# A transformer block with two mixture-of-experts FFNs on one core: the first FFN computed by chosen token-expert pairs

## The reference

```
x = x + wavelet_attention(layernorm(x))
x = x + ffn(layernorm(x))              # the FFN that the change touches
x = x + attention(layernorm(x))        # local, top-k and global keys
x = x + ffn(layernorm(x))

def ffn(x, Wg, W1, W2):                # 8 experts, D = 128, H = 256
    probs = softmax(x @ Wg); top_w, top_i = top_k(probs, 2)
    top_w = top_w / (sum(top_w) + 1e-8)
    combine = one_hot weights of the two chosen experts, else 0
    h = square(relu(einsum('td,edh->teh', x, W1)))
    y = einsum('teh,ehd->ted', h, W2)
    return einsum('te,ted->td', combine, y)
```

## Time and profile before

| | us |
|---|---|
| median of 2 runs | 679.55 (676.53 to 682.57) |
| the profiled execution | 683.03 |
| its span, first to last instruction | 681.1 |
| TensorE's mean granted clock in it, as a share of 2.4 GHz | 0.946 |

### The profile page before, as it was taken

The page is one execution under the profiler, slowest core; times in us unless marked ns, Lnnn a source line. Parts: engine busy times, 40 slices in busy tenths (PEclk is TensorE's granted clock), DMA queues, the critical chain, the costliest instruction groups (busy, mean ns, idle before and its releaser), DMA issues.

```text
span 681.1 us, 13634 instructions
## 1 busy us (share of the span) xinstructions
PE 606.3 (89%) x4874; PEld 378.8 (56%) x4874; DVE 429.0 (63%) x1449; ACT 336.5 (49%) x697; POOL 227.6 (33%) x386
## 2 busy tenths in 40 slices
PE   6799888888795866999999998999989989999997
PEld 3376566466474553555555554555445436677776
DVE  2446755744744788777777877787777536654554
ACT  5434432522431200567776667767646764445543
POOL 1121111321341309766666854787501001000000
PEclk9979999989888895799999999999989999999999
DMA  8000000000000000000000000000000000000000
GB/s 259 18 1 1 1 0 1 0 1 0 2 0 1 10 0 12 13 13 14 13 14 12 11 14 12 13 8 11 9 12 12 3 1 0 1 17 15 1 16 17
DMA packets 13171, 9.52 MB, mean 14 GB/s; under 512 B 5168, under 2 KB 12720, under 8 KB 12848
## 3 DMA queue, kind: packets, MB, share of 16 engines
q1 hardware_dynamic: 13104, 8.66, 4.5%
HBM read 4.71 MB, written 1.05 MB: 8 GB/s over the span
## 4 chain that ended last, share of the span: by engine, by line
PE 69%; DVE 23%; issue 5%; ACT 1%; POOL 1%; DMA 0%; SPq 0%; POOLq 0%; DVEq 0%; ACTq 0%
PE BANK L1079 18%; PE BANK L1064 11%; PE BANK L1223 5%; PE BANK L1174 5%; PE BANK L1198 4%; PE BANK L1195 3%; DVE X L808 3%; PE BANK L1180 3%; PE BANK L1226 2%; PE BANK L1229 2%; DVE QST L899 2%; DVE SW L852 2%; PE BANK L1201 2%; DVE M L851 2%; PE BANK L968 2%
## 5 line engine op out<-in xcount | busy, mean ns | idle before, releaser
L610 ACT ACTIVATE PT<-BANK 128x256 f32<-128x256 f32 (+2 forms) x352 | 156.9, 493 | 92.7 <-PE BANK L1198 75.3
L388 POOL TENSOR_SCALAR OH<-IOTA,POS 128x128 bf16<-128x128 bf16 x240 | 139.5, 602 | 33.3 <-DVE POS L860 28.8
L1079 PEld LDWEIGHTS BANK<-W,HID 128*128 128x128 f32 x1024 | 133.2, 206 | 28.0 <-issue 14.2
L537 ACT ACTIVATE RELU<-BANK 128x512 f32<-128x512 f32 x128 | 76.2, 596 | 141.1 <-PE BANK L1064 140.6
L808 DVE SCALAR_TENSOR_TENSOR X<-BANK,COMB,X 128x128 f32<-128x128 f32 x256 | 72.1, 344 | 116.7 <-PE BANK L1079 116.7
L1079 PE MATMUL BANK<-W,HID 128*128 128x128 f32 x1024 | 136.5, 292 | 7.6 <-DVE HID L797 7.6
L1064 PE MATMUL BANK<-XNT_ALL,W 128*128 128x512 f32 x256 | 122.8, 607 | 0.0
L894 DVE CUSTOM_DVE_ANT_0 XN_a<-BANK,BANDQ 128x256 f32<-128x256 f32 (+1 forms) x128 | 62.6, 489 | 38.9 <-PE BANK L1174 38.8
L894 DVE CUSTOM_DVE_ANT_0 XN_c<-BANK,BANDQ 128x384 f32<-128x384 f32 (+1 forms) x128 | 62.4, 488 | 9.6 <-PE BANK L1174 8.6
L1064 PEld LDWEIGHTS BANK<-XNT_ALL,W 128*128 128x128 f32 x256 | 44.8, 198 | 37.9 <-issue 28.2
L1195 PE MATMUL BANK<-BANDK,IDB 128*128 128x128 bf16 x384 | 64.2, 222 | 0.3
(11 more groups left out here) (230 smaller groups left out, 901.4 us busy)
## 6 DMA issues: line engine op xcount, KB each, us to landing
W<-w SPq DMA_DIRECT2D x2, 1024.0 KB, 8.0
X<-x SPq DMA_DIRECT2D x4, 256.0 KB, 3.1
out<-X SPq DMA_DIRECT2D x4, 256.0 KB, 2.2
RELU<-KALL SPq DMA_DIRECT2D x20, 36.0 KB, 1.9
HID<-KALL SPq DMA_DIRECT2D x20, 36.0 KB, 1.9
ROW<-rows SPq DMA_DIRECT2D x1, 320.0 KB, 3.1
RELU<-KALL SPq DMA_DIRECT2D x20, 8.0 KB, 1.7
HID<-KALL SPq DMA_DIRECT2D x20, 8.0 KB, 1.7
```

The lines of the kernel that those rows point to most:

```text
L388: last = nc.gpsimd.tensor_scalar(OH[g % 2][:, i, t, :], IOTA[:, :], POS[:, t, c:c + 1], None, ALU.is_equal)
L537: nc.scalar.activation(RELU[u % 4][:, :], UP_BANK[hh][:, :], ACT.Relu).then_inc(s["relu"], 1)
L610: nc.scalar.activation(PT[u % PT_RING][:, 0:w], P2_BANK[u % SCORE_RING][:, 0:w], ACT.Exp, scale=SCALE).then_inc(S["exp_done"], 1)
L1079: last = mm(DOWN_BANK[e % 2][:, t * P:(t + 1) * P], HID_T[e % 2][:, hh, t * P:(t + 1) * P], W2[:, e, hh, :], start=(hh == 0), stop=(hh == ...
```

## The change

The first FFN no longer loops over experts for all tokens. The sequences are taken in two waves of two. In each wave there are 2048 pairs of a token and a chosen expert.

- `choices` (DVE, step 7) writes each token's two weights into the normalised rows XROW (130 wide: 128 channels, the weight, the number of the pair); ScalarE makes the second copy of the rows. `positions` (TensorE, step 7) counts with triangular matmuls how many tokens before this one chose the same expert, `slots` (DVE, step 8) turns it into a row of the DRAM tensor XS, which has a region for each expert, and GpSimd scatters the rows there in 16 indirect DMAs a wave. `table` (DVE, step 9 of the wave's second sequence) lists for each of the 23 tiles its region row and its expert; 23 tiles of 128 rows always suffice.
- SyncE reads each tile's two numbers from SBUF into registers and loads its rows from DRAM and its expert's weights (256 KB, from SBUF to SBUF: W1 and W2 now lie together as W12) into a ring of four. A tile is then: `tile_turn` (transpose), `tile_copy`, `tile_up`, `tile_hidden` (ReLU and square, both ScalarE), `tile_down`, `tile_y` (DVE: times the weight, and the number of the pair as an index), `tile_out` (GpSimd: an indirect DMA to YT in DRAM).
- When all tiles of a wave are out, `sums_in` loads the two rows of each token, and `add_experts` adds them to X.
- The steps of `a_step` run two sequences at a time, two steps apart (`pair`): for sequences 0 and 1 ahead of wave 0; for 2 and 3 the first four ahead of it and the others beside its tiles. They share banks, so steps have new waits for the copies of the other sequence, as `pe.wait_ge(S["a_coef_s"], sent["a_coef"])` in step 0. The steps of `c_step` for sequences 0 and 1 run beside wave 1, those of 2 and 3 after it. `keep_busy` is cut to three matmuls after each pair of steps.
- At the start SyncE fills both XS with zeros, 4.33 MB each, behind the loads of the inputs.
- On GpSimd `stacks` and `values` of sequences 0 and 1 stand behind the last `tile_out`, ahead of `rstd("c", 2)`.

The second FFN and all that follows are as before. The core of the diff (the steps' new waits, `table`, `positions` and the instructions of TensorE for a tile, which are as described, are left out):

```diff
+WAVE = 2
+JT = WAVE * T
+NT = (2 * JT * P + E * (P - 1)) // P
+REGION = JT * P
+SLOTS = E * REGION + P
+ROW_W = D + 2
+UNUSED = 4096
+A_STEPS = 10
+LAG = 2
+IN_RING = 4
...
+def pair(k, b):
+    return [(s, x) for s, x in ((k, b), (k - LAG, b + 1)) if 0 <= s < A_STEPS]
...
+A_LAST = A_STEPS + LAG
+A_AHEAD = 4
+def beside_tile(i):
+    return pair(A_AHEAD + i // 2, WAVE) if i % 2 == 0 and A_AHEAD + i // 2 < A_LAST else []
+def c_beside_tile(i):
+    return [(s, b) for s, b in ((i + 3, 0), (i - 5, 1)) if (3 if b == 0 else 0) <= s <= 3 + T]
...
+            sp.wait_ge(S["act_zero1"], 1)
+            per = SLOTS * ROW_W // P
+            reps = 13
+            for w in range(B // WAVE):
+                none = QST[1][:].rearrange("p t h c -> p (t h c)").bitcast(F32)[:, 0:per // reps]
+                sp.dma_start(XS[w][:, :].rearrange("r c -> (r c)").rearrange("(p k n) -> p k n", p=P, k=reps),
+                             none.unsqueeze(1).to_broadcast([P, reps, per // reps])).then_inc(ZEROED[w], 16)
+            def tiles_in(w):
+                sp.wait_ge(S["r_table"], w + 1)
+                sp.wait_ge(S["scattered"], 16 * 2 * JT * (w + 1))
+                for n in range(w * NT, (w + 1) * NT):
+                    i, slot = n - w * NT, n % IN_RING
+                    row = sp.value_load(TABLE[0:1, w, 0, i:i + 1], min_val=0, max_val=E * JT)
+                    e = sp.value_load(TABLE[0:1, w, 1, i:i + 1], min_val=0, max_val=E - 1)
+                    if n >= IN_RING:
+                        sp.wait_ge(S["tile_y"], n - IN_RING + 1)
+                    sp.dma_start(XT_IN[slot], XS[w][:, :].rearrange("(r p) c -> p r c", p=P)[:, bass.DynSlice(row, 1), :]
+                                 .rearrange("p r c -> p (r c)")).then_inc(TILE_IN[slot], 16)
+                    sp.dma_start(WST[slot][:, :], W12[:, bass.DynSlice(e, 1), :].rearrange("p e c -> p (e c)")
+                                 ).then_inc(TILE_IN[slot], 16)
+            def sums_in(b):
+                w = b // WAVE
+                if b % WAVE == 0:
+                    for slot in range(IN_RING):
+                        sp.wait_ge(Y_OUT[slot], 16 * slot_count(slot, (w + 1) * NT))
+                if b >= 2:
+                    sp.wait_ge(S["x_sum"], b - 1)
+                for k in range(2):
+                    first = k * JT * P + b % WAVE * L
+                    sp.dma_start(YB[b % 2][k], YT[w][first:first + L, :].rearrange("(t p) d -> p t d", p=P)
+                                 ).then_inc(Y_IN[b % 2], 16)
+            for w in range(B // WAVE):
+                tiles_in(w)
+                for b in range(w * WAVE, (w + 1) * WAVE):
+                    sums_in(b)
...
+            def scatter(b, n):
+                w, j, k = b // WAVE, b % WAVE * T + n // 2, n % 2
+                if n == 0:
+                    pool.wait_ge(S["r_idx"], b + 1)
+                    pool.wait_ge(S["g_twice"], b + 1)
+                    if b % WAVE == 0:
+                        pool.wait_ge(ZEROED[w], 16)
+                nc.gpsimd.indirect_dma_start(
+                    XS[w][:, :], bass.IndirectOffsetOnAxis(ap=IDX[:, k, j:j + 1], axis=0), XROW[:, k, j, :], None,
+                    bounds_check=SLOTS - 1, oob_is_err=False).then_inc(S["scattered"], 16)
+            def tile_out(n):
+                slot = n % IN_RING
+                pool.wait_ge(S["tile_y"], n + 1)
+                nc.gpsimd.indirect_dma_start(
+                    YT[n // NT][:, :], bass.IndirectOffsetOnAxis(ap=IDY[:, slot:slot + 1], axis=0), YST[slot], None,
+                    bounds_check=2 * JT * P - 1, oob_is_err=False).then_inc(Y_OUT[slot], 16)
...
+            with_bias(1, 0).then_inc(S["a_xb"], 1)
+            consts()
+            rstd("g", 0)
+            ones()
+            rstd("g", 1)
+            rstd("a", 2)
+            pool.wait_ge(S["a_x1"], 1)
+            with_bias(2, 0).then_inc(S["a_xb"], 1)
+            for n in range(2 * T):
+                scatter(0, n)
+            for n in range(2 * T):
+                scatter(1, n)
+            rstd("a", 3)
+            pool.wait_ge(S["a_x1"], 2)
+            with_bias(3, 0).then_inc(S["a_xb"], 1)
+            rstd("g", 2)
+            for i in range(NT):
+                if i == 3:
+                    rstd("g", 3)
+                tile_out(i)
+                if 9 <= i < 9 + 2 * T:
+                    scatter(2, i - 9)
+                if 15 <= i < 15 + 2 * T:
+                    scatter(3, i - 15)
+            rstd("c", 0)
+            for i in range(NT):
+                tile_out(NT + i)
+                if i == 4:
+                    rstd("c", 1)
+            for b in range(2):
+                stacks(b)
+                if b == 0:
+                    for slot in range(IN_RING):
+                        pool.wait_ge(Y_OUT[slot], 16 * slot_count(slot, 2 * NT))
+                values(b)
             pool.wait_ge(S["a_x1"], B)
             for i in range(HG):
                 last = nc.gpsimd.memset(KZ[0][i].bitcast(F32), 0.0)
             last.then_inc(S["heads_zero"], 1)
+            rstd("c", B - 2)
...
+            def tile_copy(n):
+                act.wait_ge(S["tile_t"], n + 1)
+                nc.scalar.copy(XTS[n % 2], T_BANK[:, 0:P]).then_inc(S["tile_xt"], 1)
+            def tile_hidden(n):
+                act.wait_ge(S["tile_up"], n + 1)
+                nc.scalar.activation(TR[n % 2], U_BANK[n % 2][:, 0:HID], ACT.Relu).then_inc(S["tile_relu"], 1)
+                if n >= 2:
+                    act.wait_ge(S["tile_down"], n - 1)
+                act.wait_ge(S["tile_relu"], n + 1)
+                nc.scalar.activation(TH[n % 2], TR[n % 2], ACT.Square).then_inc(S["tile_sq"], 1)
...
+            def choices(b):
+                h = b % WAVE * T
+                ranks("g", b)
+                nc.vector.tensor_scalar(MSK[:, h:h + T, :], GR[:, :, :], 2.0, None, ALU.is_lt).then_inc(S["r_mask"], 1)
+                link(weights(GW[:, :, :]))
+                for k in range(2):
+                    link(nc.vector.scalar_tensor_tensor(out=GK[:, :, :], in0=GR[:, :, :], scalar=float(k), in1=GW[:, :, :],
+                                                        op0=ALU.is_equal, op1=ALU.mult))
+                    link(nc.vector.reduce_sum(XROW[:, k, h:h + T, D], GK[:, :, :], AX_X))
+            def slots(b):
+                h = b % WAVE * T
+                dve.wait_ge(S["r_pos"], b + 1)
+                link(nc.vector.tensor_tensor(GS[:, :, :], R_BANK[:, 0:T * E].rearrange("p (t e) -> p t e", t=T),
+                                             EBASE[:, :].unsqueeze(1).to_broadcast([P, T, E]), ALU.add))
+                for k in range(2):
+                    link(nc.vector.scalar_tensor_tensor(out=GK[:, :, :], in0=GR[:, :, :], scalar=float(k), in1=GS[:, :, :],
+                                                        op0=ALU.is_equal, op1=ALU.mult))
+                    with nc.allow_low_precision(reason="row numbers, whole and below 2 ** 24"):
+                        last = nc.vector.reduce_sum(IDX[:, k, h:h + T], GK[:, :, :], AX_X)
+                    if k == 0:
+                        link(last)
+                last.then_inc(S["r_idx"], 1)
...
+            def tile_y(n):
+                slot = n % IN_RING
+                dve.wait_ge(S["tile_down"], n + 1)
+                if n >= IN_RING:
+                    dve.wait_ge(Y_OUT[slot], 16 * (n // IN_RING))
+                nc.vector.tensor_scalar(IDY[:, slot:slot + 1], XT_IN[slot][:, D + 1:D + 2], float(UNUSED), None, ALU.add)
+                nc.vector.tensor_scalar(YST[slot], D_BANK[:, 0:D], XT_IN[slot][:, D:D + 1], None, ALU.mult).then_inc(S["tile_y"], 1)
+            def add_experts(b):
+                dve.wait_ge(Y_IN[b % 2], 32 * (b // 2 + 1))
+                x = X[:, seq(b), :]
+                link(nc.vector.tensor_tensor(x, x, YB[b % 2][0], ALU.add))
+                nc.vector.tensor_tensor(x, x, YB[b % 2][1], ALU.add).then_inc(S["x_sum"], 1)
...
+            stats("a", 3)
+            for k in range(A_AHEAD):
+                for s, b in pair(k, 2):
+                    a_step(s, b)
+                if k == 0:
+                    normalize("a", 3)
+            for i in range(NT):
+                for s, b in beside_tile(i):
+                    a_step(s, b)
+                tile_y(i)
+            for b in range(2):
+                add_experts(b)
+            for s in range(3):
+                c_step(s, 0)
+            for i in range(NT):
+                for s, b in c_beside_tile(i):
+                    c_step(s, b)
+                tile_y(NT + i)
+            for b in range(2, B):
+                add_experts(b)
+                for s in range(2):
+                    c_step(s, b)
+                if b < B - 1:
+                    for s in range(3, 4 + T):
+                        c_step(s, b)
...
+            def wave(w, beside):
+                n0 = w * NT
+                tile_turn(n0)
+                tile_up(n0)
+                tile_turn(n0 + 1)
```

(8 more changed lines are left out.)

365 lines of the change are left out of this document (255 added, 110 removed).

## The result

| | before | after |
|---|---|---|
| median of 2 runs | 679.55 | 753.86 us (752.95 to 754.76) |
| ratio, 95% interval | | 1.109 (1.087 to 1.131) |
| span of the profiled execution | 681.1 | 753.0 us |
| first MAX8 / from it to the end | 225.2 / 455.9 | 297.1 / 455.9 us |

The direction and the wide range (680 to 775) held. The point, 722, was 32 us too low, and the forecast's own narrower range (695 to 745) was missed. First the page of the changed kernel: the busy line, the granted clock in 40 slices of 18.8 us, and the shares of the chain that ended last.

What follows compares the result with a forecast made beforehand. TensorE's work was taken to bound the first FFN. First tile 72, tiles 115, steps beside 21, gap 15, end 44 sum to MAX8 at 267 us against 225.2, 42 later: 722 us predicted, range 680 to 775.

Steps and rivals of the forecast that it cites:

- the forecast's own narrower range (695 to 745): Whole kernel: the range around the predicted 722 us that the forecast itself claimed, chance 0.50.
- the gap: Between the waves: result scatter, sums' loads, adds, statistics and normalisation leave TensorE standing about 15 us.
- The period, 2.5 us: Each tile of both waves: ring and SyncE together take 2.5 us, 115 us for 46 tiles.
- ring 2.4: Tile loop: load, transpose, down, y, next load take 4.8 us for two tiles, as a ring of two.
- SyncE binds: Rival, tile loop: register loads of 1.2 us and more make 3.5 us a tile, 769 us; chance 0.14.
- loads are not in the loop: Rival, tile loop: fast loads let the period fall to ScalarE's 1.2 to 1.3 us, 666 us; chance 0.11.
- the four steps of batches 2 and 3, some 8 us: Before the first tile: the little work TensorE has during the wait for scatters and load.
- bind only from 1.9: GpSimd in wave 0: 39 indirect DMAs at 1.3 us fit; rival at 1.9 us each, 735 us, chance 0.15.
- The end: Last y to first MAX8: rstd behind stacks, values and memsets, 24.5 us; in all 44.7 against 8.8.
- Beside the tiles: Steps of other batches in the tile loop: 15 us exposed in wave 0, 6 us in wave 1.
- Zero fill free: Start: zeroing 4.33 MB a wave is done at 34 to 55 us, earlier than the last scatter.
- Clock: Waves: TensorE's granted clock falls under 0.8, adding 0.1 to 0.2 us a tile.

Runs made afterwards that it cites:

- e3: Changed kernel with the 46 tiles' rows and experts as constants, so SyncE has no register loads; DMAs the same: 742.3 us.
- e6: Changed kernel with constants for register loads, the transpose of tile i+2 behind tile_down(i), and no 256 KB weight copy: 738.1 us.
- e1: Changed kernel with the rstd of sequence 3 moved on GpSimd between the scatters of sequences 0 and 1: 747.7 us.
- e12: Changed kernel with sequence 3's eight scatters behind the last result scatter of wave 0: 761.0 us.
- e2: Changed kernel with GpSimd's work after the last tile reordered, stacks and values put around the two late rstd, memsets ahead: 744.9 us.
- e10: Changed kernel with the edits of e1, e2 and e12, one register load a tile, and the transpose of tile i+2 behind tile_down(i): 736.1 us, ratio 1.080.
- e13: The edits of e10 without that of e12, on the changed kernel: 735.4 us, ratio 1.082.

## Why the prediction held, and where it was 30 us short

The mechanism held: the FFN stopped being bound by TensorE's work, the loop around a tile ate what the smaller work saved, and the start, the gap and the end came on top. That the time fell inside the range is in part luck. Its upper end, 775, had been held open for SyncE at 3.5 us a tile (769 us); SyncE does bind, but at 2.6, and the 30 us came from elsewhere. The range that the forecast gave itself ended at 745, and the time is 9 us above it.

In the prediction's own terms, all counted from transpose to transpose or to the last y:

| term | predicted | measured | difference |
|---|---|---|---|
| first transpose of a tile | 72 | 85.6 | +13.6 |
| from it to the last y of wave 0 | 57.5 + 15 | 78.1 | +5.6 |
| to the first transpose of wave 1 | 15 | 20.3 | +5.3 |
| to the last y of wave 1 | 57.5 + 6 | 64.7 | +1.2 |
| to the first MAX8 | 44 | 48.4 | +4.4 |
| behind it | 455.9 | 455.9 | 0 |

- **The period, 2.5 us, was right (2.6), its order not.** Prediction: ring 2.4, SyncE 2.3, the register loads at 0.6 each. Measured: with all that is around them a register load is 0.8 us, so SyncE is at 2.6, and it binds, with the ring close behind at 2.3 (e3). So near a hit took two errors that in part cancel: the load too cheap, and 0.1 to 0.2 added for a clock that costs nothing here. (The ring's 2.05 goes with a landing in 2.2 us, not with the 2.5 named beside it, and by the 2.7 us that it estimates for 322 KB the sum gives 2.3, not 2.2; neither changes the forecast.) The rival "SyncE binds" had the right place and a price, 1.2 us and more, that was too high. The Trainium skill, DMA: Bandwidth & Descriptors (Latency and other measured facts), has a register load at about 600 ns at least; here the two are 0.27 and 0.53 us by themselves and 0.8 each with what goes with them. The measured times decide. The same page's 2.0 us plus bytes over 436 GB/s (Anatomy of one DMA) is its fit for DMAs that GpSimd issues; taken for these, which SyncE issues, it would have the weights land after about 2.6 us, an estimate; the median here is 2.4.
- **The rival "loads are not in the loop" is closed.** It needed 1.59 us a tile or less for no change, and had taken ScalarE's 1.2 to 1.3 us for its floor. In e6 TensorE waits for no load and a tile takes 1.97 us (2.14 with the steps beside), by the alternation of TensorE and ScalarE. The rival had taken the busy time of one engine and left out that the two take turns; and TensorE's part was 1.53 us, not 1.1.
- **The start: the step that failed is "the four steps of batches 2 and 3, some 8 us".** They were counted as hidden in the wait, since TensorE is idle there. They were not, for an `rstd` that they need stands on GpSimd behind the 16 scatters. By its load, asked for at 73.5, the first transpose would have come at 76.5 (3.0 us later, as in e1), and it came at 85.6: 9 us. e1 gives 8 back at the first transpose. TensorE's busy time between the first slot numbers and the first tile was 17.7 us, some 13 of it those steps, not 8: the granted clock was 0.60. The other 4 to 5 us are slot numbers at 48.7 in place of 45, which only this run has: ten others have 45.3 to 45.9, as predicted. The 16 scatters took as long as predicted (49.7 to 70.1, 1.28 us each against 1.3).
- **GpSimd: right on the average, wrong in the place.** 39 indirect DMAs x 1.3 are 51 us in a wave of 72: true, but 30 of them fall to the second half, which they fill. So GpSimd does bind there, at 1.28 us each, where the prediction let it bind only from 1.9. It is not the tiles that pay for that, but the last result, whose way out starts 4.5 us after its y, where 1.1 is the time without a queue (e12). In the gap's error of 5.3 us stands besides the sums' way in, 5.6 us from issue to add for 1 MB where 3.6 had been taken.
- **The end: the mechanism and its size were right**, 24.5 us predicted up to the end of the `rstd`, 25.0 measured; DVE waited the 15 us for it that were predicted. Behind it 23.4 us in place of 20.2 (the sum rounded 44.7 to 44). That is the four QKV steps: with VG they took 10.4 us where 6.9 had been taken, TensorE at the low clock with 1.62 us a step in place of 0.9. Here the clock does cost. e2 shows that 8.7 of the end go by order alone.
- **Beside the tiles**: 15 us exposed in wave 0 were about 18 (78.1 less 23 tiles at 2.6). SyncE, which waits 3 us in wave 1, waits 16 in wave 0 for results, which fits, but no experiment took the steps away; this term stays argued.
- **Zero fill free**: yes. The fill that the first scatter waits for landed at 34.5 (18.5 us after its issue), as predicted, and the scatter, at 49.7, waited for its row numbers. The second fill, for wave 1, landed at 47.1.
- **Clock**: as predicted under 0.8 in the waves (0.74 and 0.76); as a cost of 0.1 to 0.2 us a tile it does not exist while SyncE binds (2.6 us at either clock). It costs in the start and in the end, where nothing else sets the pace.

Of the 30 us over the predicted 267, 9 in the start and 3 to 4 in the gap are one engine's program order that puts work of another sequence ahead, 3.5 in the end are the low clock, 4 are slot numbers later than in other runs, and the rest is in the period, the steps beside the tiles and the sums' way in.

## What to carry to other kernels

2.8 times less expert work (46 tiles of 128 rows for 8 x 2048) did not pay, because TensorE's 137 us were one matmul behind the other from weights that stay in SBUF, and what replaced them is 46 small loops, each with DMAs, register loads and six hand-overs between engines, with a start, a middle and an end in which little overlaps. Before such a change, price one round of the loop by every engine's program order, semaphores included, and not by busy times. Then follow each small shared instruction (here `rstd`) through the queue that it stands in: the start and the gap were off by what stood on GpSimd ahead of it and of the last result. And read a single run's gain from a stretch whose length repeats (here the end, to 0.2 us), not from a point whose time moves by 5 us without an edit.

## What the runs showed of the hardware

- An indirect DMA of 128 rows holds GpSimd for 0.97 us, with 0.30 us to the next: 1.28 us each in an unbroken row, for 520 B rows and 512 B rows alike.
- The same register load costs 0.27 us for the first and 0.53 us for the second number of a pair (medians, 85 to 165 us), each followed by 0.15 us of register arithmetic; a DMA with a register in its address is issued in 0.34 us (rows) and 0.50 us (weights), against 0.33 and 0.47 with constants.
- SyncE's instruction stream can stall: on one chip, in three kernels, single instructions of 18 to 160 ns took about 700 ns each, five or six of them within 15 to 20 us. What brings it about is open.
- DVE's four normalising instructions (128x128, float32) take 1.11 us while GpSimd stands still, 2.06 with 1.2 us of GpSimd's sums or casts of 512 columns beside them and 3.10 with 2.9 us (e2, e10, e13; 3.24 with 3.2 us at 184.7 in the kernel before). Memsets beside them (at 34.0 in the kernel before) left it at 1.11.
- Four DMAs of 256 KB from DRAM issued one behind the other landed 4.2 to 5.7 us after their issues in the gap, with the first add 5.6 us after the first issue. X's four at the start of the kernel before had a median of 3.1.
